# A feed-forward, attention, feed-forward block: in a batch's last seven slots, weighted values go ahead of scores on TensorE, and additions ahead of softmax on VectorE

## The reference

```python
x = x + 0.5 * ffn(layernorm(x), w_gate, w_up, w_down)
x = x + attention(layernorm(x), Wq, Wk, Wv)
x = x + 0.5 * ffn(layernorm(x), w_gate, w_up, w_down)
# attention: one head, causal
scores = (Q @ K.T) / sqrt(256)                 # keys after the query: -inf
out = softmax(scores) @ V
# ffn: every linear layer quantizes its input and its weights to FP4 in blocks of 16
h = silu(q(x) @ q(w_gate).T) * (q(x) @ q(w_up).T)      # 704 columns
out = q(h) @ q(w_down).T
```

## Time and profile before

| | |
|---|---|
| median of 3 runs | 1227.78 us (1227.09 to 1229.02) |
| profiled execution | 1227.53 us |
| its span | 1225.4 us |
| attention, about | 414 to 881 us |
| busy share of TensorE | 95% |
| VectorE, ScalarE, GpSimd | 83%, 64%, 45% |
| mean granted clock of TensorE | 0.993 |

### The profile page before, as it was taken

One profiled execution on the slowest core, in us unless ns is written; L12 is line 12 of the kernel. 1 busy time (PEld: TensorE's weight loads), 2 busy tenths in 40 slices (PEclk: granted clock), 3 DMA queues, 4 the chain that ended last, 5 costly groups with the idle time before them and its releaser, 6 DMA issues.

```text
span 1225.4 us, 24518 instructions
## 1 busy us (share of the span) xinstructions
PE 1160.7 (95%) x7765; PEld 758.2 (62%) x7765; DVE 1012.5 (83%) x2809; ACT 789.4 (64%) x1599; POOL 555.3 (45%) x531
## 2 busy tenths in 40 slices
PE   1799999999998889999999999999999999999997
PEld 1356666666665656676677667566666666666665
DVE  6899999999999676557556654764799999999996
ACT  4678888888864444435544453665678888888862
POOL 1445544545443344435443444445344544545532
PEclk9899999999999999999999999999999999999999
DMA  6955455444444456556573656547355555555565
GB/s 208 254 95 97 85 97 96 84 89 91 90 91 80 89 114 110 106 118 106 106 130 81 119 101 120 111 90 122 59 102 115 109 115 122 114 110 113 111 124 114
DMA packets 462740, 134.35 MB, mean 110 GB/s; under 512 B 441296, under 2 KB 461904, under 8 KB 462672
## 3 DMA queue, kind: packets, MB, share of 16 engines
q1 hardware_dynamic: 454928, 125.62, 52.9%
q10 hardware_dynamic: 7744, 7.86, 2.0%
HBM read 11.34 MB, written 8.39 MB: 16 GB/s over the span
## 4 chain that ended last, share of the span: by engine, by line
PE 75%; DVE 12%; issue 4%; ACT 3%; DMA 2%; SPq 2%; POOL 1%; DVEq 0%; ACTq 0%; POOLq 0%
PE ps L1512 32%; PE ps L1471 17%; PE ps L1559 12%; PE ps L1547 10%; PE ps L1532 2%; PE ps L1525 2%; DMA arena<-arena 2%; SPq L436 2%; DVE arena L1156 1%; DVE arena L1135 1%; DVE arena L991 1%; DVE arena L987 1%; ACT arena L815 1%; DVE arena L1048 1%; DVE arena L1143 1%
## 5 line engine op out<-in xcount | busy, mean ns | idle before, releaser
L1512 PE MATMUL ps<-wguT,arena 128*128 128x512 f16 (+1 forms) x2304 | 479.5, 363 | 4.4 <-DMA arena<-arena 3.2
L1512 PEld LDWEIGHTS ps<-wguT,arena 128*128 128x128 f16 x2304 | 226.0, 98 | 224.9 <-issue 7.2
L567 POOL TENSOR_TENSOR arena<-arena 128x704 f32<-128x704 f32 x128 | 193.6, 1512 | 248.1 <-DVE arena L1000 248.1
L1471 PE MATMUL ps<-wdT,arena 128*128 128x256 f16 x2176 | 261.3, 275 | 13.8 <-DMA arena<-arena 6.8
L1471 PEld LDWEIGHTS ps<-wdT,arena 128*128 128x128 f16 x2176 | 213.6, 98 | 55.1 <-DVE x_sb L1058 9.1
L594 POOL TENSOR_TENSOR arena<-arena 128x128 f16<-128x128 f32 (+7 forms) x64 | 144.0, 2250 | 213.8 <-ACT arena L815 138.7
L824 ACT ACTIVATE arena<-ps,arena,cst 128x128 f16<-128x128 f32 (+7 forms) x64 | 80.5, 1257 | 172.1 <-DVE arena L1161 149.3
L1559 PE MATMUL ps<-arena 128*128 128x256 f16 x1632 | 188.7, 273 | 1.6 <-DVE x_sb L1174 1.6
L1547 PE MATMUL ps<-arena 128*128 128x512 f16 (+3 forms) x960 | 187.2, 347 | 0.9 <-ACT arena L815 0.9
L1559 PEld LDWEIGHTS ps<-arena 128*128 128x128 f16 x1632 | 158.8, 98 | 26.8 <-DVE x_sb L1174 2.6
L745 ACT ACTIVATE arena<-arena 128x704 int16<-128x704 f32 x128 | 100.8, 787 | 114.2 <-POOL arena L567 114.2
(11 more groups left out here) (132 smaller groups left out, 1430.0 us busy)
## 6 DMA issues: line engine op xcount, KB each, us to landing
out_dram<-x_sb SPq DMA_DIRECT2D x32, 256.0 KB, 2.7
x_sb<-in_L_attn_x_dram ACTq DMA_DIRECT2D x3, 2048.0 KB, 9.1
arena<-arena SPq DMA_TRANSPOSE x384, 3.5
arena<-arena SPq DMA_DIRECT2D x8, 256.0 KB, 2.9
arena<-arena SPq DMA_DIRECT2D x4, 512.0 KB, 3.1
x_sb<-in_L_attn_x_dram ACTq DMA_DIRECT2D x1, 1536.0 KB, 7.3
arena<-in_L_ffn_w_down_dram SPq DMA_DIRECT2D x1, 704.0 KB, 8.5
arena<-in_L_ffn_w_gate_dram SPq DMA_DIRECT2D x1, 640.0 KB, 4.5
```

The source lines that it names most:

```text
L567: g.tensor_tensor(hy[u].rearrange("p (j b) -> p b j", j=BL), h[u].rearrange("p (b j) -> p b j", j=BL), hri[u].unsqueeze(2).to_broadcast([P ...
L1471: i = nc.tensor.matmul(ps_dn[w % 2], hT[w][:, c * P:(c + 1) * P], wdT[:, k, :], start=(s == 0), stop=(s == len(DOWN_STEPS) - 1))
L1512: i = nc.tensor.matmul(psf[:, 1536 * u + lo:1536 * u + hi], xv[:, u, xl, kt, :], wguT[:, wl, lo // P:hi // P, kt, :], start=(s == 0), stop ...
```

## The change

`values_first(s)` is true for slots 9 to 15. There TensorE does the weighted values of tile s - 3 before the scores of tile s instead of after them, and VectorE the addition of tile s - 3 before the softmax of tile s instead of at the slot's end. The auxiliary product stays first in both. The other slots keep their order: in slots 16 to 18 scores still go ahead of values.

```diff
+        def values_first(s):
+
+            return 2 * GT < s < TB
...
             if aux_first(s) and not scores_first(s):
                 aux_lo_part()
+            if values_first(s):
+                add_part()
             if has_scores(s, last):
                 dve_softmax(q, s, b * NCHUNK + chunks_before(s))
...
-            if aux_first(s) and s > 2 * GT:
+            if s >= TB and aux_first(s):
                 add_part()
...
             if aux_first(s):
                 aux()
+            if values_first(s):
+                weighted_values()
             if has_scores(s, last):
...
                 pe_scores(i, q)
-            weighted_values()
+            if not values_first(s):
+                weighted_values()
             if not aux_first(s):
                 aux()
```

## The result

The changed kernel takes 1243.84 us (median of 4 runs, 1243.22 to 1244.92), against 1227.78 us before. The ratio is 1.0129, 95% interval 1.0113 to 1.0145: 16.1 us slower. The profiled execution took 1244.92 us, 17.39 us more than that of before, with a span of 1242.7 us.

The account below looks back on a forecast made before the run. TensorE, busy 95% of the span, was taken to bound the kernel. Edges 11.2 + tail 2.8 + clock 3.0 = 17.0 us on 1227.53 gave 1244.5, forecast 1244.8 with the median's 0.25; range 1236 to 1250.

Parts of the forecast that it names:

- steady slots: Slots 10 to 15: spacing of scores hardly changes, exponentials, planes and transposes keep their distance from their scores; cost 0.
- Rival E: Addition ahead of softmax delays residues; auxiliary products wait in slots 10 and 11, some 0.8 us a batch: 1248; chance 0.07.
- The shift: From slot 9 scores come one set of values later, and dependent work with them: 4.26 us by slot 15.
- the low value: Refill gated by tile 14's second transpose instead of scores 15: moves 3.93 us, so 3.5 us an edge, 10.5 in all.
- The edges: Three exits to the next batch: TensorE waits for the late key refill, 3.8 + 3.8 + 3.6 = 11.2 us.
- The tail: End of last batch: third gate/up product waits 2.5 us for L987, plus 0.3 for an addition's delay: 2.8 us.
- the 0.9 us stall: Attention stage before the change: scores (L1547) wait once for an exponential (L815), 0.9 us; forecast to stay.
- The clock: TensorE's clock drops behind two of the three edge waits, 1.5 us each: 3.0 us, ends 0 and 6.
- A: Waits at edges and tail come as forecast, but the clock stays full: 1241.8 us; chance 0.25.
- B: Clock drops at every edge and in the tail: 1247.8 us; chance 0.2.
- C: Edges hidden, refill starting when SP's queue is free rather than at scores 15; only the tail pays: 1229.6; chance 0.08.
- D: Faster: existing waits go and later scores find cover everywhere, if the refill has 4.3 us of slack: 1225.3; chance 0.05.

Follow-up runs that it names:

- the first experiment: New order in the first three batches only, last batch as in the kernel before: 1237.12 us, ratio 1.0076 to the kernel before.
- the experiment with one chunk less: Changed kernel, key chunks of tiles 13 and 15 reordered, refill of key slot 1 waiting for one chunk of scores fewer: 1242.35 us, ratio 1.0118.
- the last-batch kernel: New order in the last batch only, other batches as in the kernel before: 1230.90 us, ratio 1.0031 to the kernel before.
- the one with the third product moved: Changed kernel with the third gate/up product at the end of attention put behind the weighted values of tile 14: 1238.64 us, ratio 1.0093.
- idle products: Changed kernel with ten unread 512-column products ahead of TensorE's wait for the key refill at the three batch edges: 1238.55 us, ratio 1.0089.
- refill ahead: Changed kernel, refill waiting for one chunk fewer (tiles 13 and 15 reordered) and queued on SP before tile 14's second transpose: 1234.76 us, ratio 1.0066.

## Why the prediction was right, and where it was right for the wrong reason

**No instruction more, 0 us; steady slots, 0 us.** Held: no new wait in slots 10 to 15 in the first three batches (the first experiment). That no other engine is near its bound in attention stands in the prediction with the earlier trace rows, which are shares of the whole program; in the stretch from 414 to 881 us VectorE is busy for 294 of 467 us, so it was right. In the last batch a wait came that I had priced at 0.3 us: values 9 wait 1.52 us for the addition of tile 8, which now stands in VectorE's order behind a late residue. Rival E put such waits at the auxiliary products of every batch; there they are not.

**The shift, 4.26 us.** By the scores it held; the refill moved by 3.92, 3.93 and 4.08 us (524.08 - 2.92 - 517.24 = 3.92 at the first). That is the low value, the move of tile 14's second transpose, and the experiment with one chunk less shows that in the changed kernel this transpose, and not the scores, held the queue. The step "so it was the scores, not the queue, that let them go" does not hold: the third edge keeps its gap, 0.42 us (from 752.91 to 753.33), with the scores 1.3 us out of the way. For the kernel before no run lifts the one or the other; there too the transpose ended after the scores, 739.92 against 739.59 at the third edge. What the 0.4 to 0.6 us are by which the refill trails the transpose at the third edge and not at the others stays open.

**The edges, 11.2 us.** Measured: 6.2 us, 2.1 an edge. The step that failed is the reading of the earlier trace rows: "the last lands 2.55 us after its issue ends". The chain of waits there shows three of the four issues; its DMA piece starts at 672.91, when the fourth issue starts, not when it ends. The queue's own timeline of the kernel before has the four issues as one row:

```profile
668.44 5.74 SPq L436 DMA_TRANSPOSE arena<-arena  x4
```

They ended at 674.18, so the landing came 675.46 - 674.18 = 1.28 us after the end. I added the fourth issue twice, once in 5.71 and once in 2.55. With 1.28 the slack before was 1.7 us instead of 0.46, and an edge costs 3.8 - 1.27 - 0.34 (the low value of the shift) = 2.2 us. The changed kernel gives 531.21 - 0.14 - 529.80 = 1.27.

**The tail, 2.8 us.** Measured 3.2: new waits 1.52 + 0.77 + 2.47 less the 0.9 and 0.65 that went. So the 0.9 us stall, which I kept, did go, and a wait that I had at 0.3 was 1.5. The 2.5 us for L991 came as worked out. Place and mechanism are shown by the last-batch kernel and by the one with the third product moved.

**The clock, 3.0 us.** Two drops of three edges, as taken, 1.69 us each instead of 1.5, and one more in the tail, which the sum left at nothing: 5.1 us in the profiled execution. How many there are differs between executions with the same waits: one, two or three at the edges, nine of twelve in all; in the tail four of five, in every profiled execution that has the wait for L991 (changed kernel, idle products, one chunk less, refill ahead) but that of the last-batch kernel. The Trainium skill, "TensorE: Matmul & The Clock Gate", Part 1: The HAM clock gate, says that the gate's watching window runs free of the kernel, so that the same kernel has more or fewer slow products from run to run. The traces agree that the number varies, one to three at like waits of 2.3 to 2.5 us; that the phase decides it, no run here shows.

**The sum.** 1244.8 forecast, 1243.8 measured. The closeness owes something to chance: the edges were 5 us too dear, the clock 2.1 and the tail 0.4 too cheap, and the profiled execution carries 2.9 us that have nothing to do with the change. Corrected, the terms give 6.2 + 3.2 + 1.7 times the number of drops: 14.5 us with three. The ratio's interval is some 2 us on either side of 15.8, so nothing beyond it is left over.

**Rivals.** A (clock untouched) falls by the profile and the filler. B needs four drops; the profiled execution has three, but that of the kernel with one chunk less, whose waits are alike, has all four, so B is a matter of the execution. Its size was too dear, with edges of 3.7 us. C falls: the edges paid. D falls; its condition, 4.3 us of slack at the refill, missed with 1.7. E falls by the waits of L1538 and L1531 for residues (1.0 and 0.7 us), which both kernels have.

## What to carry to other kernels

When two steps change places, the instructions of the steady part cost nothing; price the entry and the turn back, and at each ask which transfer or queue entry was waiting for the step that now comes later. Here that was a refill of keys in SP's queue, which no line of the edit touches, with 1.7 us of slack against a shift of 4. A wait of 2 to 3 us on TensorE can cost another 1.7 us behind it. Move useful products into it; useless ones gave back a part in both kernels in which they were tried. And an order that is changed on one engine has to be changed on the engine that it feeds: either half alone cost 75 us and more.

In the chain of waits, check the issues against the queue's own timeline before adding a landing to them: a piece of the chain may start at an issue's start, and the issue is then in it already.

## What the runs showed of the hardware that was not expected

A wait of 2.3 to 2.5 us in the midst of dense work dropped TensorE's granted clock to about 0.5 in some executions and not in others, at the same place in the program (1.69 us for twelve 512-column products, or nothing): behind nine of twelve waits at the edges and four of five in the tail. Once it dropped behind a wait of 1.96 us (2.38 us for six products instead of 1.46); behind the waits of 1.22 to 1.85 us at the same place of ten other executions it did not. With products of no use in the wait, twelve products took 2.76 us at three of three edges, and in the kernel before the clock was 1.00 behind the wait that had been 4.4 us. The landing of the last of four transposes came 1.27 to 1.28 us after the end of its issue, in slot 8 and at the batch edge alike.
